# The second expert layer computed over sorted tokens

## The reference, cut to what matters

```
x = x + xattn0(norm(x), ctx)     # att0, 8 heads
x = x + ffn0(norm(x))            # ffn0, token mixing
x = x + xattn1(norm(x), ctx)     # att1, 16 heads
x = x + experts1(norm(x))        # moe1, best 2 of 8, silu gate x up, 256 hidden
x = x + xattn2(norm(x), ctx)     # att2, 8 heads
x = x + experts2(norm(x))        # moe2, best 2 of 8
x = x + xattn3(norm(x), ctx)     # att3, one head
x = x + experts3(norm(x))        # moe3, best 2 of 8 and one shared

def experts2(x):                 # moe2
    z = layernorm(x) * ln_g + ln_b
    probs = softmax(z @ rW + rb)
    w = the two largest of probs, over their sum, the other six 0
    hid = gelu(z @ W1[e] + b1[e])            # for each of 8 experts e, 256 wide
    outs = hid @ W2[e] + b2[e]
    return x + sum over e of w[e] * outs[e]
```

## Time and profile before

| | value |
|---|---|
| median of 3 runs | 861.91 us |
| profiled execution: its own time | 864.2 us |
| profiled execution: span of the trace | 862.3 us |
| mean granted clock of PE | 0.938 |

### The profile page before, as it was taken

The page is one execution under the profiler, slowest core; times in us unless marked ns, Lnnn a source line. Parts: engine busy times, 40 slices in busy tenths (PEclk is TensorE's granted clock), DMA queues, the critical chain, the costliest instruction groups (busy, mean ns, idle before and its releaser), DMA issues. The chain is left out here.

```text
span 862.3 us, 14733 instructions
## 1 busy us (share of the span) xinstructions
PE 717.4 (83%) x4784; PEld 486.7 (56%) x4784; DVE 483.3 (56%) x1392; ACT 394.5 (46%) x837; POOL 238.6 (28%) x382
## 2 busy tenths in 40 slices
PE   1487788899998777998868786899999786679998
PEld 1255565556665445565534554667777675446665
DVE  4458756776777633435566865673335334444443
ACT  2356464466765454454425555453343454222221
POOL 3344454333331261516366543100001002000000
PEclk9999999999999895999958999799999999689999
DMA  9623323332222001333272320000000200033331
GB/s 272 168 57 99 93 52 92 89 94 69 64 58 58 11 34 32 102 90 107 81 205 67 82 75 2 1 1 1 1 0 1 83 1 0 3 88 97 98 97 63
DMA packets 76320, 57.96 MB, mean 67 GB/s; under 512 B 7400, under 2 KB 70120, under 8 KB 75768
## 3 DMA queue, kind: packets, MB, share of 16 engines
q1 hardware_dynamic: 74200, 52.85, 22.3%
q0 software_dynamic: 2048, 4.20, 1.6%
HBM read 25.37 MB, written 9.24 MB: 40 GB/s over the span
## 5 line engine op out<-in xcount | busy, mean ns | idle before, releaser
L912 DVE TENSOR_REDUCE negmax<-ps 128x2 f32<-128x512 f32 x256 | 169.5, 685 | 107.0 <-PE ps L1965 106.0
L1658 ACT ACTIVATE exps<-ps 128x512 f32<-128x512 f32 x256 | 148.3, 598 | 101.0 <-PE ps L1977 96.5
L1965 PE MATMUL ps<-stack 96*128 96x256 bf16 x512 | 103.6, 297 | 36.5 <-DVE negmax L912 20.0
L1977 PE MATMUL ps<-stack 99*128 99x256 bf16 x512 | 99.8, 285 | 18.5 <-DMA stack<-maxt 14.0
L1965 PEld LDWEIGHTS ps<-stack 96*128 96x128 bf16 x512 | 47.9, 103 | 62.0 <-DVE negmax L912 35.6
L1977 PEld LDWEIGHTS ps<-stack 99*128 99x128 bf16 x512 | 43.6, 100 | 60.1 <-DMA stack<-maxt 22.7
L1993 PE MATMUL ps<-exps,values 128*32 128x256 f32 x1024 | 73.3, 403 | 1.4 <-ACT exps L1658 1.4
L2224 PEld LDWEIGHTS ps<-pack_moe,ht 128*128 128x128 f32 x512 | 62.7, 194 | 16.4 <-issue 14.6
L1294 DVE SCALAR_TENSOR_TENSOR x_sb<-ps,weights,x_sb 128x128 f32<-128x128 f32 (+1 forms) x128 | 36.0, 344 | 61.8 <-PE ps L2224 61.6
L1831 ACT ACTIVATE ht<-ps,pack_moe 128x512 f32<-128x512 f32 x64 | 43.3, 686 | 57.6 <-PE ps L2312 56.0
L2224 PE MATMUL ps<-pack_moe,ht 128*128 128x128 f32 x512 | 63.0, 277 | 0.5 <-ACT ht L1831 0.5
(11 more groups left out here) (221 smaller groups left out, 1317.0 us busy)
## 6 DMA issues: line engine op xcount, KB each, us to landing
stack<-qk_parts SPq DMA_DIRECT2D x168, 128.0 KB
stack<-weights_t SPq DMA_DIRECT2D x32, 256.0 KB, 3.2
pack_moe<-in_moe SPq DMA_DIRECT2D x1, 3076.0 KB, 16.4
outputs_moe<-y_kept SPq DMA_DIRECT2D x46, 64.0 KB
ht<-gathered SPq DMA_DIRECT2D x22, 128.0 KB
gathered<-y_kept SPq DMA_DIRECT2D x10, 256.0 KB, 3.6
pack_moe<-in_moe SPq DMA_DIRECT2D x1, 2129.0 KB
pack_moe<-in_moe SPq DMA_DIRECT2D x1, 1732.0 KB, 6.9
```

The costliest lines, as they stand in the source:

```text
L912: dve.tensor_reduce(negmax_of[b % 2][:, :, h:h + 1].rearrange("p t h -> p (t h)"), ps[:, h % 2, :].rearrange("p (t k) -> p t k", t=2), AX, ...
L1658: nc.scalar.activation(exps[:, i, :], ps[:, 2 + h % 2, :], ACT.Exp, scale=scale)\
L1965: last = pe.matmul(ps[:, h % 2, t * T:(t + 1) * T], st[0:MAXROW, h, 0, t * P:(t + 1) * P], st[0:MAXROW, h, 1, :], start=True, stop=True)
L1977: last = pe.matmul(ps[:, 2 + h % 2, t * T:(t + 1) * T], st[0:MAXROW + 3, h, 1, t * P:(t + 1) * P], st[0:MAXROW + 3, h, 0, :], start=True, ...
```

## The change

moe2 becomes sorted as moe1 is, with its own step tables. Tokens are normed in groups of 6, 2, 6 and 2 tiles and turned in six chunks; the first part's routing stands in att2's tail, its sends follow one per beat. A tile has an up matmul of 256 columns, a three-row matmul of the bias onto the same bank, a Gelu of 256 columns on ACT, two transposes, a copy on DVE, two down matmuls and a three-row matmul of the second bias. The three rows are the bias as three bf16 numbers (GpSimd splits it at moe1's start; SP moves it to three partitions behind moe2's weights; the source lies in 128 new columns of att2's pack). norm(x) is added by one operation per tile beside tiles 5 to 20. The results of tiles 0 to 7 of x are joined beside the sorted tiles 29 to 43; those of tiles 8 to 15 are fetched and joined in att3's steps 0 to 3 (`JOIN_STEPS`). att3 is normed per four tiles: the first group beside sorted tiles 36 to 40, the others in steps 0, 2 and 4. The loads of att3's context chunks move with them. moe3's weights are loaded when the last sorted tile has been multiplied. The dense code and the hardware loop go.

```
-SORTED = ("moe1",)
-EXPERT = {"moe1": 768}
+SORTED = ("moe1", "moe2")
+EXPERT = {"moe1": 768, "moe2": 512}
...
-NORMED = (range(0, 8), range(8, 14), range(14, NT))
-CHUNKS = ((0, 1, 2, 3), (4, 5, 6, 7), (8, 9, 10, 11), (12, 13), (14, 15))
+NORMED = {"moe1": (range(0, 8), range(8, 14), range(14, NT)), "moe2": (range(0, 6), range(6, 8), range(8, 14), range(14, NT))}
+CHUNKS = {"moe1": ((0, 1, 2, 3), (4, 5, 6, 7), (8, 9, 10, 11), (12, 13), (14, 15)),
+          "moe2": ((0, 1, 2, 3), (4, 5), (6, 7), (8, 9, 10, 11), (12, 13), (14, 15))}
+TURN_BANKS = {"moe1": (4, 4, 0, 1, 5), "moe2": (4, 4, 4, 0, 1, 5), "att3": (6, 0, 0, 0), "moe3": (0, 1, 0, 6)}
...
-SORT_STEPS = {"stats": ((-1, 3), (2, 3)), "rstd": ((-1, 4), (2, 4)), "norm": ((-1, 8), (2, 6)), "logits": (-1, 15),
-              "top": (0, 1), "exp": (0, 2), "first": (0, 4), "second": (0, 6), "mark": (0, 8), "rank": (0, 9),
-              "place": (0, 11), "weigh": (1, 12), "load": (2, 6)}
-TURN_STEPS = ((-1, 10), (-1, 12), (2, 13), (2, 15))
-TURNED_STEPS = ((-1, 11), (-1, 13), (3, 0), (3, 1))
-SEND_FROM = 14
+SORT_STEPS = {
+    "moe1": {"stats": ((-1, 3), (2, 3)), "rstd": ((-1, 4), (2, 4)), "norm": ((-1, 8), (2, 6)),
+             "turn": ((-1, 10), (-1, 12), (2, 13), (2, 15)), "turned": ((-1, 11), (-1, 13), (3, 0), (3, 1)),
...
+    "moe2": {"stats": ((-2, 5), (-1, 5), (2, 5)), "rstd": ((-2, 7), (-1, 7), (2, 5)), "norm": ((-1, 0), (0, 0), (3, 5)),
+             "turn": ((-1, 2), (-1, 4), (0, 1), (3, 5), (3, 6)), "turned": ((-1, 3), (-1, 5), (0, 2), (3, 6), (3, 7)),
+             "logits": (0, 2), "top": (0, 3), "exp": (0, 4), "first": (0, 5), "second": (0, 6), "mark": (0, 7), "rank": (1, 0),
+             "place": (1, 1), "weigh": (1, 3), "load": (2, 3), "logits2": (3, 7)}}
+SEND_FROM = {"moe1": 14, "moe2": 9}
+SEND_EVERY = {"moe1": 2, "moe2": 1}
...
+JOIN_TILES = {"moe1": (30, 32, 33, 34, 36, 38, 40, 42), "moe2": (29, 31, 33, 35, 37, 39, 41, 43)}
+PLUS_TILES = range(5, 5 + NT)
+JOIN_STEPS = {0: (8,), 1: (9, 10, 11), 2: (12,), 3: (13, 14, 15)}
+LAST_TILES = {"stats": 36, "norm": 39, "turn": 40}
...
+            def pass_tiles(s):
+                for j in range(ALL_TILES + AHEAD):
+                    if j < ALL_TILES:
+                        load_tile(s, j)
+                    if j >= AHEAD:
+                        store_output(s, j - AHEAD)
...
                         sp.dma_start(pack["moe2"][:, 0:cols["moe2"]], args["moe2"]).then_inc(loaded["moe2"], 16)
+                        sp.wait_ge(bias_split, 5)
+                        for k in range(3):
+                            sp.dma_start(bias_rows[k:k + 1, :], split[:, k, :]).then_inc(bias_in, 16)
...
-            def plus_norm(s, g):
-
-                tiles = GROUPS[s][g]
-                wait(dve, "zt_psum", s, 0, tiles[-1] // BT)
-                for t in tiles:
-                    last = dve.tensor_scalar(z[:, t, :], x_sb[:, t, :], moments[:, t, 0:1], rstd[:, 1, t:t + 1],
-                                             ALU.subtract, ALU.mult)
-                last.then_inc(sem["x_plus"], 1)
-                wait(dve, "x_plus", s, 0, g)
-                for t in range(tiles[0], tiles[-1], BT):
...
+            def keep_of_norm(s):
+
+
+                r1 = rstd[:, 1, :]
+                dve.tensor_scalar(keep[:, 0, :], r1, 1.0, None, ALU.add).then_inc(sem["x_plus"], 1)
+                dve.scalar_tensor_tensor(out=keep[:, 1, :], in0=moments[:, :, 0], scalar=-1.0, in1=r1, op0=ALU.mult, op1=ALU.mult)\
+                    .then_inc(sem["x_plus"], 1)
+                wait(dve, "x_plus", s, 0, 1)
+
+            def plus_norm(s, t):
+
+                dve.tensor_scalar(x_sb[:, t, :], x_sb[:, t, :], keep[:, 0, t:t + 1], keep[:, 1, t:t + 1], ALU.mult, ALU.add)\
+                    .then_inc(sem["x_plus"], 1)
 
...
-GROUPS = {s: PART if s in SORTED else (range(0, NT - BT), range(NT - BT, NT)) for s in ("moe1", "moe2", "att3", "moe3")}
+GROUPS = {"moe1": PART, "moe2": PART, "att3": tuple(range(t, t + BT) for t in range(0, NT, BT)),
+          "moe3": (range(0, NT - BT), range(NT - BT, NT))}
...
-                stats_all(s, 1, GROUPS[s][1])
-                apply_all(s, 1, GROUPS[s][1])
                 for step in range(B + 2):
                     p, m, d = step, step - 1, step - 2
+                    if step == 0:
+                        apply_all(s, 1, GROUPS[s][1])
...
+                    if step in (2, 4):
+                        apply_all(s, step // 2 + 1, GROUPS[s][step // 2 + 1])
                     if valid(d):
                         wait(dve, "proj_psum", s, d)
                         wait(dve, "xb_ready", s, d)
                         dve.tensor_tensor(x_sb[:, 2 * d:2 * d + 2, :], ps[:, 6, 0:2 * D].rearrange("p (t c) -> p t c", t=2),
                                           xb[:, :, :], ALU.add).then_inc(sem["x_updated"], 1)
+                    if step in JOIN_STEPS:
+                        for t in JOIN_STEPS[step]:
+                            join_outputs("moe2", t)
+                    if step in (1, 3):
+                        stats_all(s, step // 2 + 2, GROUPS[s][step // 2 + 2])
...
                     wait(pool, "taken_psum", s, 0, SEND_TILE + n * 9 // 10)
                 else:
-                    done_heads = SEND_FROM + 2 * n - COL_BEAT[16]
-                    wait(pool, "cols_psum", "att" + s[3:], B - 2 + done_heads // 16, done_heads % 16)
+                    flow = "att" + s[3:]
+                    done_heads = SEND_FROM[s] + SEND_EVERY[s] * n - COL_BEAT[H[flow]]
+                    wait(pool, "cols_psum", flow, B - 2 + done_heads // H[flow], done_heads % H[flow])
...
             def sorted_tiles(s):
 
 
-                make_rstd_all(s, len(NORMED) - 1, NORMED[-1])
+                make_rstd_all(s, len(NORMED[s]) - 1, NORMED[s][-1])
+                if s == "moe1":
+                    split_biases()
                 for t in GROUPS[s][1]:
                     for k in range(2):
                         send_row(s, 1, t, k)
                 for t in range(2 * FETCHED_EARLY):
                     for k in range(2):
                         fetch_output(s, t, k)
-                    if t == 5:
+                    if s == "moe1" and t == 5:
                         make_rstd(EARLY[0], 0, False)
...
+            def split_biases():
+
+
+                pool.wait_ge(loaded["att2"], 16)
+                whole = par("att2", "later", 4 * E)
+                pool.tensor_copy(split[:, 0, :], whole).then_inc(bias_split, 1)
+                pool.wait_ge(bias_split, 1)
+                pool.tensor_tensor(split_rest, whole, split[:, 0, :], ALU.subtract).then_inc(bias_split, 1)
+                pool.wait_ge(bias_split, 2)
+                pool.tensor_copy(split[:, 1, :], split_rest).then_inc(bias_split, 1)
+                pool.wait_ge(bias_split, 3)
+                pool.tensor_tensor(split_rest, split_rest, split[:, 1, :], ALU.subtract).then_inc(bias_split, 1)
+                pool.wait_ge(bias_split, 4)
+                pool.tensor_copy(split[:, 2, :], split_rest).then_inc(bias_split, 1)
 
             for s in STAGES:
...
+                    for t in range(2 * FETCHED_EARLY, NT):
+                        for k in range(2):
+                            fetch_output("moe2", t, k)
+                        if t == 11:
+                            add_bias(s, 0)
+                        if t == 13:
+                            make_rstd_all(s, 2, GROUPS[s][2])
+                            add_bias(s, 1)
+                    add_bias(s, 2)
+                    make_rstd_all(s, 3, GROUPS[s][3])
+                    for d in range(3, B):
                         if d == B - 2:
                             make_rstd_all("moe3", 0, GROUPS["moe3"][0])
                         add_bias(s, d)
...
                         pe.wait_ge(sem["h_ready"], done("h_ready", s, 0, j - 1)) if j >= 1 else None
                         at = weights_at[j + 1]
-                        pe.matmul(ps[:, (j + 1) % 2, :], taken_t[:, (j + 1) % 2, :], par(s, "experts")[:, bass.ds(at, 2 * T)],
-                                  start=True, stop=True).then_inc(sem["up_psum"], 1)
+                        w = up_width(s)
+                        last = pe.matmul(ps[:, (j + 1) % 2, 0:w], taken_t[:, (j + 1) % 2, :],
+                                         par(s, "experts")[:, bass.ds(at, w)], start=True, stop=(s == "moe1"))
+                        if s == "moe2":
+                            last = pe.matmul(ps[:, (j + 1) % 2, 0:w], ones16[0:3, :], bias_rows[:, bass.ds(at, w)],
+                                             start=False, stop=True)
+                        last.then_inc(sem["up_psum"], 1)
                         if j + 1 + REGISTERS < ALL_TILES:
                             load_experts(s, slice(j + 1 + REGISTERS, j + 2 + REGISTERS))
...
                         for c in range(2):
                             last = pe.matmul(ps[:, 4, 0:D], turned[:, (j - 1) % 2, c * P:(c + 1) * P],
```

(6 more changed lines are left out.)

545 lines of the change are left out of this document (235 added, 310 removed), and 3 rows, old and new, of the table PACKS.

## The result

The changed kernel takes **928.63 us** (median of 4 runs, 923.78 to 930.47); the kernel before took 862.97 beside it. The ratio is 1.076 (95% interval 1.070 to 1.082): slower by 66 us, where 24 us faster was forecast. The profiled execution is the fastest of the four, 923.78 us with a span of 922.0, 59.7 more than before.

What follows compares the result with a forecast made beforehand. The prediction took PE as the bound, with dense moe2 computing all eight experts for every token. −129.9 + 16 + 82 + 8 = −23.9 took the profiled run to 840.3, so 838 us by the median; eight-in-ten range 822 to 860.

Steps and rivals of the forecast that it cites:

- the term for the 46 sorted tiles: Sorted moe2 stage on PE: start 17, 40 tiles at 1.40 us 56, pauses 5, last tile 4; 82 us added.
- the fourth rival: PE stays at 1.2 GHz through moe2's tiles: 1.36 us more each, kernel 900; chance 0.07 including an unseen stall.
- the bare loads: In moe2's tiles, both bias matmuls' weight loads covered by nothing: tile 1.57 us, stage 8 us longer, kernel 845.
- The bounds: Steady moe2 tile on PE: 1.36 us if nothing else binds, 1.56 with uncovered bias loads, 1.63 at moe1's pace.
- The sum of the moving columns: Steady moe2 tile on PE from moe1's tile: 1.63 − 0.43 + 0.11 + 0.05 = 1.36 us.
- The front: Before moe2: routing, places, then 16 sends; last send at 558, first tile near 563, not 546.75; +16 us.
- The stage: The second expert layer over 46 sorted tiles, from its start to the last down matmul: 82 us.
- The last attention: att3: fetches of tiles 8 to 15 in steps 0 to 3, mostly beside the steps; +8 us.
- The sum: Whole kernel: −129.9 for the dense stage, +16 front, +82 sorted tiles, +8 last attention; −23.9 us.

Runs made afterwards that it cites:

- the paced run: The changed kernel with bias matmuls over 128 rows of ones and six more copies per tile on DVE; 931.09 us, ratio 1.079.
- the burst run: The changed kernel with 16 more f32 matmuls of 512 columns on PE behind tile 8 of the second expert layer; 883.28 us, ratio 1.035.
- e9_three_rows: The changed kernel itself, unedited, run once more on another chip (C); 929.46 us, ratio 1.076.
- e11_16_rows: The changed kernel with bias matmuls of ones times ones over 16 rows in place of three; 929.46 us, ratio 1.076.

## Why the prediction was wrong

**The step that failed** is the clock of the tiles in the term for the 46 sorted tiles, 82 us forecast and 152.9 measured. "PE stays at the 1.2 GHz level through the tiles" stood as the fourth rival (0.07 for it and an unseen stall together), argued away with "moe1's tiles, of the same form". They were not of the same form: what moe1's tiles don't have, the three-row bias matmuls, is what kept the clock at 0.50 for all but the last two of 46 tiles. With 128 rows in their place and nothing else in the tile changed in size, the clock is 1.00 and the stage 79 us. The rival's figure was good, 1.36 us a tile forecast and 1.39 measured, but that is the price of the lower level whatever holds it there. Its reason was not: waits between tiles don't hold the clock low, as the paced run shows. Its total of 900 was 29 short of the median; it left the bare loads out, 0.5 us a tile or some 23 us in all.

**The second miss** is the size of the bias matmuls' loads. The bounds ran to 1.56 us a tile, one bare load of 98 ns for each; measured at full clock the tile is 1.88, 0.50 over the 1.38 without gaps, since the full-height loads behind them are bare as well, and at the lower clock the gaps are 0.55 of 3.27. The sum of the moving columns itself was right: 1.36 forecast, 1.38 with 128 rows. So was the Trainium skill's rule, "TensorE: Matmul & The Clock Gate", section "LDWEIGHTS (loading the stationary operand)": a load's time goes by its columns, so three rows take as long as 128. The traces agree to 8 ns, with a median of 90 ns for three rows and 98 for 128, both at a clock of 1.00 (the burst run and the run with 128 rows). What it does to the loads beside it, the rule doesn't say.

**The front** was right in mechanism and 3 us short: sends one after another from the places on. The last send was 1.7 us late (559.69 for 558), and from the load to the first tile 3.9 us passed where 2.5 were allowed. The pause of 8.46 us on ACT lay mostly beside the sends: take the 8.3 us of pauses in moe1's tiles off, and the first tile would have stood at 557.6, an estimate, where on chip A, without pauses, it stood at 554.9 to 557.6. It cost 3 us at most. The pauses in moe1's tiles aren't in the +19 either, for the kernel before has 9.2 us of them there.

**The stage**, with the clock at 1.00, was 79 us with 128 rows on chip A (first transpose 555.0 to the last bias matmul at 633.4) where 82 were forecast. On a chip with pauses it is longer by some 15.

**The last attention** is a term that was mis-sized: 8 forecast, 17 measured. The forecast put it on the fetches; without any fetch 13 us remain. Of the norm per four tiles it counted the roots on GpSimd (2 × 1.0) and left out the copies on ACT and the turn on PE, which stand among a step's work: 2 to 3 us are shown for the copies. The rest isn't assigned.

**The sum** with these sizes and full clock would have been −129.9 + 19 + 79 + 17 = −15 us, which is what the run with 128 rows gave on chip A (837.85 against 853.38, −15.5) and no other chip did. The agreement to 1 us has some luck in it, since 19 and 17 are from a chip with pauses and 79 is from A.

## What to carry to other kernels

Before a small matmul is added to a dense stream, look at its height and not only at its columns: a few rows of bias cost 0.05 to 0.11 us of columns and brought 0.5 us of bare weight loads and half the clock; filling it up to 128 rows with zeros took both away and adds no columns, though the zeroing has a price of its own (here 3.5 us on GpSimd, in which DVE came to a near stop). When a stage is taken as the model for another, list what the new one has that the model lacks, and ask of each whether the model's clock still holds. And time a version on more than one chip: the same program was 1.8% faster than its rival on one (a single run) and 0.8% slower on another.

## What the runs showed of the hardware that was not expected

- With bias matmuls of 3 rows in bf16, 16 rows in bf16 or 1 row in f32 in each tile the granted clock stayed at 0.50 for 134 us and more of PE busy without a break (206 with the f32 row); with 32, 64 or 128 rows it was 1.00 from 12 to 14 us after the first tile, and also with 128 rows while PE waited for DVE 40% of the time, there from 24 us. Tiles with three rows kept a clock of 1.00, for some 70 us, that a burst of full-height f32 matmuls had raised. In the changed kernel it rose at 710.1, 4 us after the start of four full-height transposes for att3 (L1931, 706.23), and 3.5 us after them in `e9_three_rows` and `e11_16_rows`; with the f32 row it didn't. That these transposes raised it isn't shown.
- A matmul of 32 or 64 rows among full-height ones makes its own load and the next full-height load wait for the matmul ahead: 1.88 us a tile in place of 1.38. The matmuls of 96 and 99 rows in att2, next to each other, showed no such gap (two of 256 columns in 0.22 us).
- A MEMSET of 3.50 us on GpSimd held two operations on DVE that began beside it until it ended: 3.53 us where they take 0.73.
- Pauses, counted once where engines coincide, came to 22 to 36 us a profile in the edited kernels on three chips, to 17 in the changed kernel and 9 in the kernel before, and to none in the four profiles on chip A. They stand at much the same places of the program each time, in sorted tiles above all; their cause is open.
